# Sort pass of a graph kernel: edge network products two pairs of tiles apart, its input side one group ahead on its own PSUM bank, one-hots and record weights in other places

## The reference, cut to what matters

```python
h = silu(edge_attr_64 @ W_fc1 + b_fc1)
h = silu(h @ W_fc2 + b_fc2)
w = h @ W_fc3 + b_fc3
tp = (msg_src[src] + msg_dst[dst]) * edge_weight1 * w
...
e_contrib = edge_attr_16 @ a_edge
```

## Time and profile before

| what | value |
| --- | --- |
| median of 3 runs | 18235.65 us (18226.8 to 18244.18) |
| profiled execution, its own time | 18221.89 us |
| profiled execution, span | 18220.2 us |
| the second pass of the sort | 518 to 5614.6 us of the span |
| TensorE over the span | 10937.8 us (60%) |
| VectorE over the span | 10051.8 us (55%) |
| GpSimd over the span | 8943.4 us (49%) |
| mean granted TensorE clock | 0.665 |

### The profile page before, as it was taken

How to read it: one execution, slowest core, us unless ns; L and a number is a source line. 1 busy time by engine, 2 the same in 40 slices (tenths; PEclk the granted TensorE clock), 3 DMA queues, 4 the chain that set the end, 5 groups by cost and what they waited for, 6 DMA issues and landing times. The chain is left out here.

```text
span 18220.2 us, 324915 instructions
## 1 busy us (share of the span) xinstructions
PE 10937.8 (60%) x72618; PEld 8416.8 (46%) x72619; DVE 10051.8 (55%) x34887; ACT 4411.8 (24%) x12105; POOL 8943.4 (49%) x9494
## 2 busy tenths in 40 slices
PE   6555555555553666666497466664456774556886
PEld 5333333333332555555387344443235664335886
DVE  9555555555552233333386477775247553666787
ACT  0111111111110122222211144102420111545775
POOL 0466566655663455555677344554530443443443
PEclk9777666766675666666655556776566655556998
DMA  9622222222223222222432399875664889444655
GB/s 369 233 64 66 63 66 66 63 65 63 65 64 74 49 58 58 58 58 58 73 68 52 65 311 310 262 236 170 203 223 130 235 236 168 125 128 149 198 196 155
DMA packets 2203667, 2437.44 MB, mean 134 GB/s; under 512 B 1038593, under 2 KB 1838538, under 8 KB 2203506
## 3 DMA queue, kind: packets, MB, share of 16 engines
q1 hardware_dynamic: 1817174, 1665.89, 33.0%
q0 software_dynamic: 345088, 579.41, 10.4%
q10 hardware_dynamic: 41244, 190.45, 2.7%
HBM read 1589.15 MB, written 845.52 MB: 134 GB/s over the span
## 5 line engine op out<-in xcount | busy, mean ns | idle before, releaser
L565 POOL DMA_INDIRECT edges_by_dst<-rec,pos x1568 | 1524.9, 972 | 2011.7 <-DVE rec L500 1541.7
L988 POOL DMA_INDIRECT sc_rows<-src_table,sc_idx x1664 | 1582.1, 951 | 1422.2 <-DVE sc_tp L1086 770.4
L565 POOL DMA_INDIRECT edges_by_cell<-rec,pos x1568 | 1530.9, 976 | 528.5 <-issue 527.3
L1758 PE MATMUL ex_rows<-table,ex_oh 128*128 x6528 | 1127.3, 345 | 991.9 <-issue 292.1
L1038 PE MATMUL sc_loc<-dst_table,sc_ohT 128*128 x3328 | 760.4, 400 | 1093.3 <-ACT sc_ohT L1004 1033.2
L1758 PEld LDWEIGHTS ex_rows<-table,ex_oh 128*128 128x128 bf16 x6528 | 764.0, 132 | 1355.0 <-issue 1312.2
L529 DVE SCALAR_TENSOR_TENSOR junk<-rowb,keycol,earlier 128x128 f32<-128x128 f32 (+1 forms) x3136 | 1149.2, 415 | 168.0 <-issue 163.5
L1097 DVE TENSOR_TENSOR sc_qk<-sc_loc,sc_kv 128x256 f32<-128x256 f32 x416 | 176.7, 425 | 1917.0 <-ACT sc_kv L1017 1368.1
L1038 PEld LDWEIGHTS sc_loc<-dst_table,sc_ohT 128*128 128x128 f32 x3328 | 654.7, 293 | 1232.6 <-issue 1232.5
L542 DVE SCALAR_TENSOR_TENSOR junk<-look,onehot 128x128 f32<-128x128 f32 x3136 | 738.4, 287 | 826.9 <-remote 480.0
L1851 PE MATMUL gs_part<-gs_rows,gs_oh 128*128 128x192 bf16 x6528 | 917.2, 292 | 432.7 <-DVE gs_oh L1822 214.1
(11 more groups left out here) (423 smaller groups left out, 28076.3 us busy)
## 6 DMA issues: line engine op xcount, KB each, us to landing
ex_keys<-src_key_rows SPq DMA_DIRECT2D x1632, 128.0 KB
gs_rows<-dst_rows_by_src SPq DMA_DIRECT2D x1088, 192.0 KB
rowb<-sort_key_rows SPq DMA_DIRECT2D x392, 512.0 KB
ex_keys<-dst_key_rows SPq DMA_DIRECT2D x1088, 128.0 KB
dst_rows_by_src<-patY ACTq DMA_DIRECT2D x1, 104448.0 KB
rows_by_src<-ex_stage SPq DMA_DIRECT2D x544, 192.0 KB
scored_dst_rows_by_src<-patZ ACTq DMA_DIRECT2D x1, 70720.0 KB
turned_rows_by_src<-ex_stage SPq DMA_DIRECT2D x544, 128.0 KB
```

The source lines that it names most:

```text
L565: nc.gpsimd.indirect_dma_start(out=out, out_offset=bass.IndirectOffsetOnAxis(ap=pos[:, u, k, j:j + 1], axis=0), in_=row, in_offset=None).t ...
L988: nc.gpsimd.indirect_dma_start(out=rows[:, u, j, :], out_offset=None, in_=tabS, in_offset=bass.IndirectOffsetOnAxis(ap=idx[:, u, j:j + 1], ...
L1758: m = nc.tensor.matmul(rows[k][u % deep][r // 2][:, r % 2, 0:W], oh[k][:, u % deep, r * P:(r + 1) * P], t3[:, bass.ds(held[k][u], 1), :].r ...
```

## The change

The edge network gets two kinds of PSUM banks instead of one: `xin` for its input side (transposes, fc1) and `xout[u]` for fc2 and fc3. The input side of group g + 1 is worked during group g. On TensorE, fc2 of group g and the transposes of group g + 1 stand behind pair 0; the one-hots' turning behind pair 1; bias and fc3 of group g and fc1 of group g + 1 behind pair 2; nothing behind pair 3. ScalarE's order follows. VectorE makes four of the next group's six one-hot pieces at the start of a group and two behind pair 0. `weights(g, u)` reads the same group's output and stands at the end of the group, so GpSimd waits for `s_rec` of g + 3. SyncE loads attributes three groups ahead (`ea`) and two (`ea16`), each on its own semaphore, and now waits in group g for the scatters of group g - 1. `w1` loses eight unused columns.

```diff
-        xps = [ps(f"xps{u}", [P, 512]) for u in range(2)]
+        xin = ps("xin", [P, 512])
+        xout = [ps(f"xout{u}", [P, 512]) for u in range(2)]
...
+                def load_rows(g, u):
+                    for k in range(2):
+                        at = krow[k, 0:1, 0:1]
+                        sp.dma_start(rowb[:, u, k, :, :].rearrange("p t e -> p (t e)"),
+                                     bass.AP(tensor=at.tensor, offset=at.offset + g * (SG * P), ap=[[0, P], [1, SG * P]])).then_inc(s_rb[u], 16)
+
+                def load_attr(g, u, hi):
+                    for low, high in ((0, 112), (112, hi)):
+                        sp.dma_start(ea[low:high, u, :, :], ea_v(low, high, g)).then_inc(s_ea[u], 16)
+
+                def load_attr16(g, u, hi):
+                    for low, high in ((0, 112), (112, hi)):
+                        sp.dma_start(ea16[low:high, u, :, :], ea16_v(low, high, g)).then_inc(s_e16[u], 16)
+
+                def step(i, his, first, last):
                     for u in range(2):
                         g = i * 2 + u
-                        if after is not None:
-                            sp.wait_ge(s_pick, (after * 2 + u + 1) * PAIRS + LOOKS)
-                        for k in range(2):
-                            at = krow[k, 0:1, 0:1]
-                            sp.dma_start(rowb[:, u, k, :, :].rearrange("p t e -> p (t e)"),
-                                         bass.AP(tensor=at.tensor, offset=at.offset + g * (SG * P), ap=[[0, P], [1, SG * P]])).then_inc(s_rb[u], 16)
-                        if after is not None:
-
-                            sp.wait_ge(s_xt, after * 2 + u + 1)
-                            sp.wait_ge(s_p16, after * 2 + u + 1)
-                        for lo, hi in ((0, 112), (112, rows_hi)):
-                            for buf, view in ((ea, ea_v), (ea16, ea16_v)):
-                                sp.dma_start(buf[lo:hi, u, :, :], view(lo, hi, g)).then_inc(s_ea[u], 16)
-                        if after is not None:
-
-                            sp.wait_ge(s_sc[u], (after + 1) * 2 * SG * 16)
+
+                        sp.wait_ge(s_xt, g + 2)
+                        load_attr(NG - 2 if last and u == 1 else g + 3, 1 - u, his[u])
+                        sp.wait_ge(s_pick, (g + 1) * PAIRS + LOOKS)
+                        load_rows(g + 2, u)
+                        sp.wait_ge(s_p16, g + 1)
+                        load_attr16(g + 2, u, his[0])
+
+                        if not (first and u == 0):
+                            sp.wait_ge(s_sc[1 - u], (i + u) * (2 * SG * 16))
                             sp.sem_inc(s_free, 1)
...
                 def weights(g, u):
-                    v = 1 - u
                     dve.wait_ge(s_m3, g + 1)
-                    nc.vector.tensor_tensor(rec[:, v, :, 0:C], xps[v][:, :].rearrange("p (t c) -> p t c", c=C),
+                    nc.vector.tensor_tensor(rec[:, u, :, 0:C], xout[u][:, :].rearrange("p (t c) -> p t c", c=C),
                                             bcast(w1[:, bass.ds(g * SG, SG)], 2, [P, SG, C]), ALU.mult).then_inc(s_rec, 1)
+
...
                         g = i * 2 + u
-
-                        dve.wait_ge(s_ea[u], (i + 1) * 64)
+                        for part in range(HALF0):
+                            onehots(g + 1, 1 - u, part)
+                        dve.wait_ge(s_e16[u], (i + 1) * 32)
                         nc.vector.tensor_tensor(prod16[:, :, :], ea16[:, u, :, :], bcast(a16[:, :], 1, [P, SG, 16]), ALU.mult).then_inc(s_p16, 1)
...
                             m.then_inc(s_pick, 1)
-                            for part in (2 * c, 2 * c + 1):
-                                if part < NK:
+                            if c == 0:
+                                for part in range(HALF0, NK):
                                     onehots(g + 1, 1 - u, part)
-                            if c == 1:
-                                weights(g, u)
+                        weights(g, u)
                         dve.wait_ge(s_pick, (g + 1) * PAIRS + LOOKS)
                         nc.vector.tensor_tensor(pos[:, u, :, :], cnt[:, u, :, :], sel[:, u, :, :], ALU.add).then_inc(s_pos, 1)
-                weights(NG, NG % 2)
 
             @block.gpsimd
             def _(pool):
...
-                        pool.wait_ge(s_rec, g + 4)
+                        pool.wait_ge(s_rec, g + 3)
...
+                def take_attr(g):
+                    act.wait_ge(s_xt, g + 1)
+                    nc.scalar.copy(eaT[:, :], xin[:, :]).then_inc(s_xc, 1)
+
+                def first_layer(g):
+                    act.wait_ge(s_m1, g + 1)
+                    nc.scalar.activation(h1[:, :], xin[:, :], ACT.Silu, bias=bb[:, 0:1]).then_inc(s_h1, 1)
...
+                take_attr(0)
+                first_layer(0)
                 with act.Fori(0, NG // 2) as i:
                     for u in range(2):
                         g = i * 2 + u
                         v = 1 - u
-                        act.wait_ge(s_xt, g + 1)
-                        nc.scalar.copy(eaT[:, :], xps[u][:, :]).then_inc(s_xc, 1)
-                        act.wait_ge(s_m1, g + 1)
-                        nc.scalar.activation(h1[:, :], xps[u][:, :], ACT.Silu, bias=bb[:, 0:1]).then_inc(s_h1, 1)
+                        act.wait_ge(s_m2, g + 1)
+                        nc.scalar.activation(h2[:, :], xout[u][:, :], ACT.Silu, bias=bb[:, 1:2]).then_inc(s_h2, 1)
+                        take_attr(g + 1)
 
                         act.wait_ge(s_pick, g * PAIRS + LOOKS)
                         keycols(g + 1, v)
                         turn_copy(g + 1, v)
-                        act.wait_ge(s_m2, g + 1)
-                        nc.scalar.activation(h2[:, :], xps[u][:, :], ACT.Silu, bias=bb[:, 1:2]).then_inc(s_h2, 1)
+                        first_layer(g + 1)
...
+                def turn_attr(i, v):
+
+                    pe.wait_ge(s_ea[v], (i + 1) * 32)
+                    for q in range(SG // 2):
+                        m = nc.tensor.transpose(xin[:, q * P:(q + 1) * P],
+                                                ea[:, v, 2 * q:2 * q + 2, :].rearrange("p t c -> p (t c)"), K.ident[:, :])
+                    m.then_inc(s_xt, 1)
+
+                def first_layer(g):
+                    pe.wait_ge(s_xc, g + 1)
+                    nc.tensor.matmul(xin[:, :], w1d[:, :], eaT[:, :], start=True, stop=True).then_inc(s_m1, 1)
...
                             if c == 0:
-                                pe.wait_ge(s_ea[u], (i + 1) * 64)
-                                pe.wait_ge(s_rec, g + 2)
-                                for q in range(SG // 2):
-                                    m = nc.tensor.transpose(xps[u][:, q * P:(q + 1) * P],
-                                                            ea[:, u, 2 * q:2 * q + 2, :].rearrange("p t c -> p (t c)"), K.ident[:, :])
-                                m.then_inc(s_xt, 1)
+                                pe.wait_ge(s_h1, g + 1)
+                                pe.wait_ge(s_rec, g + 1)
+                                nc.tensor.matmul(xout[u][:, :], w2d[:, :], h1[:, :], start=True, stop=True).then_inc(s_m2, 1)
+                                turn_attr(i + u, v)
                             if c == 1:
                                 pe.wait_ge(s_one, (g + 1) * NK + 2)
                                 turn(g + 1, v)
-                                pe.wait_ge(s_xc, g + 1)
-                                nc.tensor.matmul(xps[u][:, :], w1d[:, :], eaT[:, :], start=True, stop=True).then_inc(s_m1, 1)
                             if c == 2:
-                                pe.wait_ge(s_h1, g + 1)
-                                nc.tensor.matmul(xps[u][:, :], w2d[:, :], h1[:, :], start=True, stop=True).then_inc(s_m2, 1)
-                            if c == 3:
                                 pe.wait_ge(s_h2, g + 1)
-                                nc.tensor.matmul(xps[u][:, :], K.ones[0:1, :], b3[0:1, :], start=True, stop=False)
+                                nc.tensor.matmul(xout[u][:, :], K.ones[0:1, :], b3[0:1, :], start=True, stop=False)
                                 for q in range(SG // 2):
-                                    m = nc.tensor.matmul(xps[u][:, q * P:(q + 1) * P], h2[:, q * P:(q + 1) * P], w3d[:, :],
+                                    m = nc.tensor.matmul(xout[u][:, q * P:(q + 1) * P], h2[:, q * P:(q + 1) * P], w3d[:, :],
                                                          start=False, stop=q == SG // 2 - 1)
                                 m.then_inc(s_m3, 1)
+                                first_layer(g + 1)
```

46 lines of the change are left out of this document (31 added, 15 removed).

## The result

The changed kernel takes 18052.97 us (median of 4 runs, 18043.12 to 18067.65), the kernel before 18231.22 us (4 runs, 18212.49 to 18244.18): a ratio of 0.9904, 95% interval 0.9887 to 0.9921, or 178 us less. The forecast was 18335 us, 104 us more: its sign was wrong. The profiled executions are 18221.89 and 18047.96 us.

What follows compares the result with a forecast made beforehand. GpSimd was taken as bound by VectorE's group, and VectorE by the fast time around each scatter burst. Terms -14 + 113 - 41 + 41 + 0 = +99 us on the profiled 18221.9 gave 18321, as median 18335; range 17940 to 18660.

Steps and rivals of the forecast that it cites:

- The slow stretch: Second pass: after about 9.5 us of unbroken scatters other engines' signals come late, until some 2.5 us after the last scatter.
- joined burst: GpSimd's scatter burst starting with no gap after another: claimed 27, never leaving the slow stretch, mean 16.1 us gap behind each.
- Record weights, 0 us: Weights moved to the group's end: VectorE still does one whole group between starts, only the phase moves; 0 us.
- One-hots, -14 us: Four one-hots ahead of pair 0 need nothing of TensorE, so they run in a slow stretch: 27 x -0.5 = -14 us.
- Edge network, +113 us: TensorE's fc3 and fc1 ahead of pair 3 make four late signals instead of three: ordinary gaps 5.3 against 4.5, +113 us.
- Bursts after the pause, -41 and +41: After GpSimd's pauses, 7 of 27 joined pairs fall apart, -41 us; 7 ordinary bursts newly find VectorE ready, +41 us.
- Loads, 0 us: SyncE's row and attribute loads, each behind its own signal: gain lost again in the slow stretch; 0, bounds 0 and -60.
- 2: Rival: fewer waits inside TensorE bring pair 3 forward, ordinary gaps 3.1-4, some joined bursts fall apart; -240, 18000 us; chance 0.25.
- 1 (GpSimd the bound): Rival: GpSimd's bursts join and VectorE keeps up; gaps shrink from 1064 us to 196 x 0.3; 17230 us; chance 0.08.
- 3: Rival: the change gives and takes the same; the phase moves, the gap stays 4.5; 18235 us; chance 0.17.
- 5: Rival: more bursts join, each second one standing in the slow stretch; +430 us, 18665, half with half joined; chance 0.10.
- 6: Rival: pair 2 is also pending at the slow stretch's end; +250 to +522 us, 18490 to 18760; chance 0.12.

Runs made afterwards that it cites:

- m3_half_scatters: Changed kernel without the scatters into edges_by_cell, 8 a group instead of 16, so its output is incomplete; ratio 0.8855 to the kernel before.
- m2_mid_break: Changed kernel with three memsets of a spare tile on GpSimd after the 8th scatter of each burst; ratio 0.9722 to the kernel before.
- e4_weights_end_only: Kernel before with only the record weights moved to the end of their own group; ratio 0.9932 to the kernel before.
- e3_onehots_back: Changed kernel with the one-hots back in three pairs of pieces behind pairs 0, 1 and 2; ratio 0.9966 to the kernel before.
- e7_fc1_last: Changed kernel with fc1 of the next group behind pair 3, no longer ahead of pair 3's look-up; ratio 0.9928 to the kernel before.
- e6_network_only: Changed kernel with record weights and one-hots both undone, leaving the edge network's new order and the loads; ratio 0.9966 to the kernel before.
- e5_weights_and_onehots: Kernel before with record weights and one-hots moved as in the change, edge network, banks and loads as before; ratio 0.9933 to the kernel before.
- p1_nops: Kernel before with 64 instructions that do nothing on each of the five engines ahead of the second pass; ratio 0.9996 to the kernel before.
- p2_two_semaphores: Kernel before with two unused semaphores, as many as the change adds; ratio 1.0001 to the kernel before.
- m4_end_break: Changed kernel with three memsets of a spare tile on GpSimd behind the 16th scatter of each burst; ratio 0.9775 to the kernel before.
- m1_midwait: Changed kernel in which GpSimd waits after the 8th scatter until those eight have landed; ratio 0.9794 to the kernel before.
- m6_before_mid_break: Kernel before with three memsets on GpSimd in the middle of each burst; ratio 0.9789 to the kernel before.
- the pair of set 3: Kernels before and after, unaltered, run once more and profiled on one chip; ratios 1.0001 and 0.9910 to the kernel before.
- m5_mid2: Changed kernel with two memsets of a spare tile on GpSimd after the 8th scatter of each burst; ratio 0.9797 to the kernel before.

## Why the prediction was wrong, step by step

Two terms of the sum failed, and either of them alone turns its sign: the record weights, taken at 0 us, measured -124 (99 - 124 = -25), and the edge network, taken at +113, measured -62 by itself (99 - 113 - 62 = -76).

**The slow stretch** held, with its start near 9.5 us, its end about 2.5 us after the last scatter, and the long gap behind a joined burst. That VectorE never works in a joined burst was read from one; a first pair got through in 16 of 30. One thing it left out: in the stretch instructions come late for which the profile shows no wait for another engine. In the joined burst after, the second to fourth product of one pair, which need nothing new, start after 1.3 to 2.0 us of idle time:

```profile
2330.03 0.29 DVE L569 SCALAR_TENSOR_TENSOR junk<-look,onehot 128x128 f32<-128x128 f32 x1 [1.31 <-issue]
...
2333.54 0.29 DVE L569 SCALAR_TENSOR_TENSOR junk<-look,onehot 128x128 f32<-128x128 f32 x1 [2.00 <-issue]
...
2335.63 0.29 DVE L569 SCALAR_TENSOR_TENSOR junk<-look,onehot 128x128 f32<-128x128 f32 x1 [1.29 <-issue]
```

The prediction weighed this against the Trainium skill, SBUF — State Buffer, section "Who interferes with whom", by which TensorE and ScalarE wait for nobody. That section speaks of ports of the SBUF, and the unchanged 0.284 and 0.291 us of VectorE's products do not speak against it; what the prediction drew from it, that there would be no late signals, does not hold. m3_half_scatters and m2_mid_break agree with the rows: with the same work on all other engines the group takes 15.6 us beside bursts of 10.2 us and 25.3 beside bursts of 20.5, and 3.3 us without a scatter in each burst take the ratio from 0.9904 to 0.9722.

**Record weights, 0 us.** This step failed. It reasoned that VectorE must do one whole group between two starts, so that only the phase moves. True, but a group is not all alike: a slow stretch falls on whatever TensorE and ScalarE hand each other at that phase. e4_weights_end_only measured -124 us for it (0.9932), and TensorE's wait for the first silu ahead of fc2 falls from 767.6 us in the trace before to 38.2 in it (weight loads).

**One-hots, -14 us.** The sign was right, the size off: -60 us (0.9967). The step looked at what the one-hots wait for (nothing of TensorE) and not at who waits for them: TensorE's turning, 1057 us of waits in e3_onehots_back, 67 after. On top of the weights' move alone they gave nothing (0.9933 against 0.9932).

**Edge network, +113 us.** This step failed too. "VectorE reaches pair 1's end near 8.0 us" was 6.4. The path of 8.0 was counted from `pos`, and the burst starts 0.9 us after it; the other 0.7 us are terms taken too long. At 6.4 pair 2 fits into fast time as well (9.0), and only pair 3 is left behind the edge. The count itself was wrong as well. fc3's and fc1's signals go to VectorE's last step and to ScalarE; they do not stand one behind another ahead of pair 3. e7_fc1_last took fc1's away, and pair 3 came no earlier. The ordinary gap was taken at 5.3 against 4.5; it is 3.95 against 4.32. It has two sizes. Before, 58 of 134 are 3.3 us (the last pair was through before GpSimd stopped) and 76 are 5.1 (it was not). After, 65 of 139 are 3.5 and 74 are 4.3. The share hardly changed. The late gap shrank by 0.8 us, in two like parts (medians): the last pick ends 2.9 us after the stop against 3.4, and from there to the next burst it is 1.6 us against 2.1, where two one-hots no longer stand. The update had come before the stop in all 74 (57 of 76 before), the case that the prediction put at 4.8. e6_network_only alone did have 4.8 us: for the network's part without VectorE's parts the step had its direction right in ordinary gaps, and missed the 1.2 us behind joins (14.4 against 15.6) and the seven joins fewer (23 against 30) that pay for it. On top of the weights' move alone the network's part does cost time, 0.9966 against 0.9932 (62 us), with fc2's wait for the silu at 484.3 us against 38.2.

**Bursts after the pause, -41 and +41.** The joins went from 31 to 28 (the prediction read 27 of 31, since four are put down to other releasers than "issue"). What it held fixed, the 16.1 us behind each, is what moved: 13.75. Pair 0 now gets through inside the joined burst in 28 of 28, and the three pairs left come 2.5 and 3.2 us apart (medians), without one-hots between them; before, the last three came 4.3 and 3.2 us apart.

**Loads, 0 us.** Nothing contradicts it. The pass of e5_weights_and_onehots, with the old loads, equals that of the kernel after. The loads were not moved by themselves.

**The rest of the program** was not in the sum at all; 52 of the 174 us lie there. In each of the three sets that hold both kinds, the kernels with the network's part have less outside than those without: 13263 and 13265 against 13297 and 13328, 13089 and 13089 against 13129 and 13139, 13281 and 13291 against 13361 and 13342. It is not the number of instructions ahead nor the semaphores' numbers, by p1_nops and p2_two_semaphores. But m4_end_break, with the network's part, has 40 us more outside than m1_midwait and m2_mid_break of the same set (13323 against 13281 and 13283), and on another chip m6_before_mid_break, without it, has 13287. These are single profiles: two of the kernel before, on two chips, have 13145 and 13129. The difference does not lie right behind the pass. Over the first 5000 us behind it the traces before and after stay within 5 us of each other, and 11200 us behind it they are 50 apart; the pair of set 3 does the same (7 and 36 us). What in the network's part does it stays open; the order of PSUM banks and the programs' own lengths were not tried.

**The rivals.** 2 gave 18000 us, at a chance of 0.25, and 18053 came; its sign, ordinary gaps under 4, was just met (3.95). Its sum was right by luck in part: it took 1.0 us off each ordinary gap and 14 joins apart, where 0.37 us and 3 joins came, and the shorter gaps behind joins and the 52 us outside were not in it. Its reason, fewer waits inside TensorE, is half the matter: those waits did go, but VectorE's parts remove them without any change of order on TensorE. 1 (GpSimd the bound) did not come by the change; with the break in the burst it nearly does, at 24.0 us a group. 3, 5 and 6 did not come: pair 2 is through by 12.4 us of every ordinary burst, and joins did not multiply. The range, 17940 to 18660, held the time.

## What to carry to other kernels

When one engine's stream makes the others late after some microseconds, try its start where what follows in the group has the fewest hand-overs between engines; "only the phase moves" is no argument for a cost of zero. Price parts together as well as one by one: here a part gave, did nothing, or cost, by which others were there. Of work that is moved, ask who waits for it as well as what it waits for, and count a late signal only if the engine that waits for it is on the path. A short break in the stream (here 3.3 us in the middle of 20) can be worth more than every reordering around it.

## What the runs showed of the hardware

- 16 indirect scatters issued by GpSimd at 1.26 us each run the other engines freely for about the first 9.5 us; after that their signals, and their own next instructions, start 1 to 6 us late (up to 25 us in a joined burst, kernel before), until about 2.5 us after the stream stops. An instruction that has started takes as long as ever (0.284 and 0.291 us). A break of 3.3 us in the middle ends it nearly (gaps of 0.61 us in m2_mid_break); one of 2.2 us does so only in part (2.23 us in m5_mid2).
- GpSimd pauses 2.0 to 2.2 us at every 112th scatter (behind the first one of every seventh burst of 16, 27 times in 3136), in the traces before and after and in all others without a break in the middle; in m3_half_scatters too, with 13 times in 1568.
- Code that a change does not touch can move by 0.4% with it: 13145 to 13094 us outside the pass (single profiles), from a cause that two tests did not find.
